# Batch 0's prologue: the second weight-block sum ahead of two token statistics, x's second block ahead of the means' spread

## The chip, the cores and the metric

One Trainium2 chip, one core of it. The metric is the device time of one execution in microseconds (us), the median of several runs. Five engines work side by side, each through its own instruction stream in order: TensorE (PE: matmuls, with PEld for its weight loads), VectorE (DVE), ScalarE (ACT), GpSimd (POOL) and SyncE (SP, which here only issues DMAs). They meet through semaphores: an instruction waits until a semaphore has reached a number, and everything behind it on its engine waits with it.

## What is computed

x has 16 batches of 512 tokens with 512 features. Four normalised or shifted copies of x are scaled, joined to 3072 features per token and put through a two-layer net, whose normalised output is added to x:

```python
h = _ln(x, pw_g[pathway_ids], pw_b[pathway_ids])
h = _ln(h, cp_g[compartment_ids], cp_b[compartment_ids])
t = _ln(x, tm_g[time_steps], tm_b[time_steps])
m = x + _mlp_ln(memory_state, ...)[:, None, :]      # n, r alike, from noise_state, resource_state
s = _ln(x, ms_g[scale_type], ms_b[scale_type])
w = jax.nn.softmax(aw)
cat = jnp.concatenate([w[0]*h, w[1]*t, w[2]*m, w[3]*n, w[4]*r, w[5]*s], axis=-1)
return x + _mlp_ln(cat, int_W1, int_b1, int_W2, int_b2, int_g, int_be)
```

Since m, n and r all hold x itself, the kernel adds up their three blocks of int_W1, weighted with w, into one block that multiplies x.

## The kernel before

Every large matmul is made of float32r operands split in a high and a low part, three matmuls for one product (high by high, high by low, low by high). The features of the joined input come in 16 rows of 128, k = 0 to 15. Rows 0 to 3 are x with the summed weights, the rest are t, s and h. A batch is one turn of `chunk`; batch 0 has a `first_chunk` of its own on each engine, in which the weights are also loaded, summed, scaled and split. The order on each engine is the order in which its code is written out; no scheduler moves anything.

The part that the change touches is the first 30 us of batch 0. What works there on what:

- **The weight sum of block k** (k = 0 to 3, 128 rows each). The three source blocks land in `keep`. ACT's `sum_first(k)` (L691) scales the first of them, DVE's `sum_blocks(k)` (L1149, two instructions) adds the other two, ACT's `sum_high(k)` (L695) rounds the sum to the high part `w1_hi` and DVE's `sum_low(k)` (L1141) takes the rest, `w1_lo`.
- **x turned, in two halves** (two feature rows each). ACT's `x_high(0, i)` (L771) rounds the half i, DVE's `x_low(0, i)` (L936) takes the rest.
- **x's product in block k** on PE: `x_high_part(k)` is four matmuls on x's high part (L1573) and four on its low part (L1576), and waits for `sum_high(k)`; `x_low_part(k)` (L1582, four) waits for `sum_low(k)`.
- **The token statistics of batch 0.** DVE's `x_stats(0, t)` for t = 0 to 3 (L929 and L932) gives mean and variance of the tokens; POOL's `x_rstd(0)` (L520, L522) makes the reciprocal deviations `xrs` once all four are there. ACT puts the means on a diagonal in `mean_diagonal` (L730, four instructions, waits for all four statistics) and the deviations in `dev_diagonal` (L736, waits for `xrs`); DVE's `high_diagonal` (L1124) also waits for `xrs`. PE spreads both over the partitions, `mean_first` (L1557) and `dev_first` (L1562, L1565).
- **What follows from them.** DVE's `scaled_first` (L969) needs `dev_first`; PE's `first_fill(0)` (L1467) needs `scaled_first` and the class table, which ACT rounds and signs (L822, L824) and DVE's `tab_low` (L1136) completes; DVE's `centre_tile(f)` (L960) needs `mean_first`.
- `warm(n)` (L1552) is n matmuls of 128 columns whose result nobody reads, with `WARM = (24, 7)` for the two places where they stand.

Behind `x_low_part(3)` PE goes on with three small nets (`nets_hidden` L1410, `nets_output` L1435), whose weight tiles SP loads through six staging buffers (L428), each released by the matmul that read the tile before it. In the trace the summed weights `w1_raw`, `w1_hi` and `w1_lo` are named w_raw, w_hi and w_lo.

Of the kernel before, what the change touches and what calls it, by code (L numbers as in the profile page):

```python
# [9 lines left out]
TT = TOKENS // P  # L10
# [17 lines left out]

FILLS0, FILLS = 2 * FT + 2, 4

WARM = (24, 7)

# [8 lines left out]
def build(nc, x, xp, xT, ids, pid, small, small_at, tabs, rows, net_vecs, pw, cp, W1s, W2s, int_W1, int_W2, out):  # L43
# [15 lines left out]
    with ExitStack() as ctx:  # L59
# [285 lines left out]
        def by_tiles(cols):  # L345

            return cols.rearrange("q (g t i) -> q t g i", t=TT, i=32)
# [336 lines left out]
        def _(act):  # L684
# [4 lines left out]
            def sum_first(k):  # L689
                act.wait_ge(sum_in[k], 16)  # L690
                act.activation(w1_raw[:, k, :], keep[:, NETS * k, :], ACT.Copy, scale=w_mix[:, 2:3]).then_inc(sum_begun, 1)  # L691
# [34 lines left out]
            def mean_diagonal():  # L726

                act.wait_ge(xaggr, TT)
                for t in range(TT):
                    act.activation(by_tiles(mean_on)[:, t, :, :], ident.rearrange("q (g i) -> q g i", i=32), ACT.Copy,  # L730
                                   scale=xmv[:, t, 0:1]).then_inc(mean_diag, 1)

            def dev_diagonal():
                act.wait_ge(xrs_done, 1)
                for t in range(TT):
                    ins = act.activation(by_tiles(dev_on)[:, t, :, :], ident.rearrange("q (g i) -> q g i", i=32), ACT.Copy,  # L736
                                         scale=xrs[:, t:t + 1])
                ins.then_inc(dev_diag, 1)
# [28 lines left out]
            def x_high(b, i):  # L767
                act.wait_ge(xT_half_in if isinstance(b, int) and b == 0 and i == 0 else xT_in, 16 * (b + 1))

                wait(act, used, 6 * (b - 1) + 5 + i)  # L770
                act.activation(cat_hi[:, slot(i), :, :], xc[:, 2 * i:2 * i + 2, :], ACT.Copy).then_inc(x_hi_done, 1)  # L771
# [42 lines left out]
            sum_high(0)  # L814
            sum_first(1)
            x_high(0, 1)
            mean_diagonal()
            sum_high(1)
            sum_first(2)
            dev_diagonal()  # L820
            act.wait_ge(table_in, 16)
            act.activation(class_tab[:, :], tab_raw, ACT.Copy).then_inc(tab_rounded, 1)  # L822
# [97 lines left out]
        def _(dve):  # L920
# [5 lines left out]
            def x_stats(b, t):  # L926
                if t == 0:
                    dve.wait_ge(x_in, 16 * (b + 1))
                dve.bn_stats(xst[:, t, :], x_sb[:, t, :]).then_inc(xstat, 1)  # L929
                dve.wait_ge(xstat, TT * b + t + 1)  # L930
                dve.nop(nofuse=True)
                dve.bn_aggr(xmv[:, t, :], xst[:, t, :]).then_inc(xaggr, 1)  # L932
# [194 lines left out]
            def high_diagonal():  # L1127

                dve.wait_ge(xrs_done, 1)
                dve.nop(nofuse=True)  # L1130
                diagonal(dev_high, xrs[:, :]).then_inc(high_diag, 1)

            def tab_low():
                dve.wait_ge(tab_hi_done, 1)

                dve.scalar_tensor_tensor(class_tab[:, :], tab_raw, tab_rest, class_tab[:, :].bitcast(f32),  # L1136
                                         ALU.mult, ALU.add).then_inc(tables_ready, 1)
# [6 lines left out]
            def sum_blocks(k):  # L1144
                dve.wait_ge(sum_begun, k + 1)
                if k == 0:
                    dve.wait_ge(sum_more_in[k], 16)
                for j in (1, 2):
                    dve.scalar_tensor_tensor(w1_raw[:, k, :], keep[:, NETS * k + j, :], w_mix[:, 2 + j:3 + j], w1_raw[:, k, :],  # L1149
                                             ALU.mult, ALU.add).then_inc(sum_done, 1)  # L1150
                    dve.wait_ge(sum_done, 2 * k + j)
# [66 lines left out]
            def first_chunk():  # L1218
                class_columns()
                sum_blocks(0)  # L1220
                x_low(0, 0)
                sum_low(0)
                for t in range(TT):
                    x_stats(0, t)
                sum_blocks(1)
                x_low(0, 1)
                high_diagonal()
                sum_low(1)
                sum_blocks(2)
                tab_low()  # L1230
                sum_low(2)
                scaled_first()
                centre_tile(0)
                sum_blocks(3)
                ts_mult(0, 0)
                sum_low(3)
                w_low(4)
                w_low(5)
                ts_low(0, 0)
                centre_tile(1)  # L1240
                ts_mult(0, 1)
                w_low(6)
                w_low(7)
                centre_tile(2)
                ts_low(0, 1)
                onehot_first()
                centre_tile(3)
                w_low(8)
                w_low(9)

                dve.wait_ge(tables_ready, 1)
                y_mul(0, 0)
                y_mul(0, 1)
                ts_mult(0, 2)
                y_mul(0, 2)
                y_mul(0, 3)
                ts_low(0, 2)
                w_low(10)
                w_low(11)
                y_add(0, 0)  # L1260
                ts_mult(0, 3)
                y_add(0, 1)
                ts_low(0, 3)
                y_add(0, 2)
                y_add(0, 3)
                w_low(12)
                for t in range(TT):
                    y_norm(0, t)
                for t in range(TT):
                    x_stats(1, t)  # L1270
                w_low(13)
                h_low(0, 0)
                nets_stats()
                w_low(14)
                w_low(15)
                turn_stats(1)
                h_low(0, 1)
                class_rows()
                nets_norm()
                x_low(1, 0)  # L1280
                x_low(1, 1)
                for t in range(TT):
                    y_mul(1, t)
                onehot_next(1)
                centre(1)
                scaled_next(1)
                y_add(1, 0)
                y_add(1, 1)
# [115 lines left out]
        def _(pe):  # L1404
# [149 lines left out]
            def mean_first():  # L1554

                pe.wait_ge(mean_diag, TT)
                pe.matmul(mean_ps, sel_all, mean_on, start=True, stop=True).then_inc(mean_spread, 1)  # L1557

            def dev_first():

                pe.wait_ge(dev_diag, 1)
                pe.matmul(dev_ps, sel_all, dev_on, start=True, stop=False)  # L1562
                pe.wait_ge(sel_ready, 3)
                pe.wait_ge(high_diag, 1)
                pe.matmul(dev_ps, sel_less, dev_high, start=False, stop=True).then_inc(dev_spread, 1)  # L1565
# [12 lines left out]
            def x_low_part(k):  # L1578
                hi = cat_hi[:, slot(k // 2), k % 2, :]
                pe.wait_ge(sum_lo_done, k + 1)  # L1580
                for h in range(FT):
                    ins = pe.matmul(hid_ps[:, h, :], w1_lo[:, k, h * P:(h + 1) * P], hi, start=False, stop=False)  # L1582
                if k % 2:
                    ins.then_inc(used, 1)
# [49 lines left out]
            def first_chunk():  # L1634
                pe.wait_ge(sel_ready, 1)
                warm(WARM[0])
                x_high_part(0)
                x_low_part(0)
                warm(WARM[1])
                mean_first()  # L1640
                x_high_part(1)
                x_low_part(1)
                dev_first()
                x_high_part(2)
                first_fill(0)
                x_low_part(2)
                x_high_part(3)
                x_low_part(3)
                nets_hidden()
                first_fill(1)  # L1650
                pair(0, 2)
                nets_hidden_turn()
                first_fill(2)
                pair(0, 3)
                first_fill(3)
                for i in range(6):
                    nets_output(i)
                pair(0, 4)
                pair(0, 5)
                for i in range(6, NETS * FT):  # L1660
                    nets_output(i)
                fill_h(0, 0)
                for i in range(6):
                    class_sum(i)
                fill_h(0, 1)
                for i in range(6, MODS):
                    class_sum(i)
                last_pairs(0, 0)
                nets_turn()
                last_pairs(0, 1)  # L1670
                for i in range(NETS * FT):
                    batch_sum(i)
                last_pairs(0, 2)
                batch_turn()
                last_pairs(0, 3)
# [120 lines left out]
```

## Time and profile before

| what | value |
|---|---|
| median of 3 runs | 944.74 us (943.46 to 945.62) |
| the profiled execution's own time | 943.69 us |
| its span, first to last instruction | 942.0 us |
| mean granted TensorE clock | 0.998 of full speed |
| PE busy | 930.0 us, 99% |
| DVE busy | 803.6 us, 85% |
| ACT, POOL busy | 276.4 us, 437.8 us |

The span is counted from the first instruction to the last; 1.7 us of the execution's own time lie around it. Busy time of PE counts matmuls back to back, with modelled ends. The clock column of the profile gives the TensorE clock that was granted, as a share of full speed. Times in the trace are microseconds from the start of the span.

### The profile page before, as it was taken

The numbers are of one execution on the slowest core, as the hardware profiler recorded it, in microseconds if no ns is written. First come the engines' busy times: TensorE is split into PE (matmuls) and PEld (weight loads), VectorE is DVE, ScalarE is ACT, GpSimd is POOL, SyncE is SP. The second block draws the span as 40 slices with busy tenths as digits, with TensorE's granted clock in tenths as the row PEclk, the third lists the DMA queues.
The fourth block names the chain that finished last, engine by engine and source line by source line (L and its number), as shares of the span: only waits on it lengthen the run. The fifth ranks groups of instructions, "written<-read, shape, count | busy, mean of one in ns | idle before, by whom it ended". The sixth has DMA issues, their size and how long they took to land.

```text
span 942.0 us, 13618 instructions
## 1 busy us (share of the span) xinstructions
PE 930.0 (99%) x4219; PEld 747.7 (79%) x4219; DVE 803.6 (85%) x1171; ACT 276.4 (29%) x353; POOL 437.8 (46%) x620
## 2 busy tenths in 40 slices
PE   8999999999999999999999999999999999999996
PEld 7677887878888787887878888787888878788785
DVE  7989998888888888888988889888888888888665
ACT  5635133241321313231241412323132231323211
POOL 3355463554445364454545346355444536445022
PEclk9999999999999999999999999999999999999999
DMA  9974677657475674856667475664847567475331
GB/s 324 368 266 148 204 178 233 180 148 232 132 231 138 235 178 118 246 149 212 155 184 218 115 243 140 228 179 139 233 141 228 139 224 185 119 239 150 87 84 64
DMA packets 98994, 174.56 MB, mean 185 GB/s; under 512 B 11552, under 2 KB 50464, under 8 KB 95008
## 3 DMA queue, kind: packets, MB, share of 16 engines
q0 software_dynamic: 22976, 66.07, 28.6%
q1 hardware_dynamic: 44032, 91.87, 28.1%
q10 hardware_dynamic: 31968, 16.39, 6.0%
q8 instruction: 9, 0.15, 0.1%
q14 instruction: 9, 0.07, 0.0%
HBM read 141.54 MB, written 32.75 MB: 185 GB/s over the span
## 4 chain that ended last, share of the span: by engine, by line
PE 94%; DVE 2%; DMA 2%; SPq 0%; issue 0%; ACT 0%; POOL 0%; DVEq 0%; POOLq 0%
PE hid_ps L1515 25%; PE hid_ps L1516 24%; PE hid_ps L1517 24%; PE o_ps L1616 3%; PE o_ps L1614 3%; PE made_ps L1616 3%; PE made_ps L1614 3%; PE made_ps L1615 3%; PE o_ps L1615 3%; PE made_ps L1467 1%; DMA stage_more<-res_W 1%; DMA keep<-int_W 1%; DVE w_raw L1149 1%; PE hid_ps L1522 0%; SPq L428 0%; PE o_ps L1435 0%
## 5 line engine op out<-in xcount | busy, mean ns | idle before, releaser
L1515 PE MATMUL hid_ps<-cat_hi,w_hi 128*128 128x512 f32 x1008 | 396.6, 393 | 0.0
L1516 PE MATMUL hid_ps<-cat_lo,w_hi 128*128 128x512 f32 x1008 | 392.7, 390 | 0.0
L1517 PE MATMUL hid_ps<-cat_hi,w_lo 128*128 128x512 f32 x1008 | 392.4, 389 | 0.0
L1515 PEld LDWEIGHTS hid_ps<-cat_hi,w_hi 128*128 128x128 f32 x1008 | 189.1, 188 | 49.8 <-issue 11.1
L1517 PEld LDWEIGHTS hid_ps<-cat_hi,w_lo 128*128 128x128 f32 x1008 | 189.2, 188 | 40.2
L1516 PEld LDWEIGHTS hid_ps<-cat_lo,w_hi 128*128 128x128 f32 x1008 | 189.3, 188 | 38.2
L567 POOL DMA_INDIRECT pw_rows<-pw,path_now x64 | 89.9, 1405 | 117.9 <-DVE y_sb L1055 101.8
L775 ACT ACTIVATE cat_hi<-v_ring 128x1024 fp32r<-128x1024 f32 x64 | 66.7, 1059 | 132.7 <-issue 77.9
L588 POOL DMA_DIRECT2D r_sb<-x x60 | 56.7, 946 | 101.4 <-DVE r_sb L1118 92.9
L574 POOL DMA_INDIRECT pw_rows<-cp,class_now x64 | 79.3, 1239 | 35.8 <-DVE y_sb L1030 18.7
L801 ACT ACTIVATE z_sb<-hid_ps,batch_bias 128x512 f32<-128x512 f32 x64 | 43.9, 692 | 168.3 <-PE hid_ps L1517 168.3
L1014 DVE TENSOR_TENSOR cat_lo<-v_ring,cat_hi 128x1024 fp32r<-128x1024 f32 x64 | 76.7, 1200 | 8.0 <-ACT cat_hi L775 8.0
L783 ACT ACTIVATE cat_hi<-v_ring 128x1024 fp32r<-128x1024 f32 x30 | 31.9, 1062 | 170.2 <-DMA v_ring<-h_turned 170.2
L520 POOL TENSOR_TENSOR fve<-fmv,eps_col 128x1 f32<-128x1 f32 x64 | 23.7, 370 | 108.7 <-DVE fmv L1074 96.2
L771 ACT ACTIVATE cat_hi<-xc 128x1024 fp32r<-128x1024 f32 x32 | 33.9, 1061 | 136.8 <-PE hid_ps L1517 136.3
L1118 DVE SCALAR_TENSOR_TENSOR r_sb<-o_sb,frs,rows_bc 128x512 f32<-128x512 f32 x60 | 45.7, 762 | 24.1 <-issue 13.4
L1009 DVE TENSOR_TENSOR v_ring<-made_ps,xc 128x1024 f32<-128x1024 f32 x34 | 41.5, 1221 | 28.3 <-PE made_ps L1467 28.2
L522 POOL TENSOR_TENSOR frs<-fve,minus_half 128x1 f32<-128x1 f32 x64 | 53.3, 833 | 5.0
L1036 DVE SCALAR_TENSOR_TENSOR y_sb<-y_sb,xrs,pw_rows 128x512 f32<-128x512 f32 x64 | 47.6, 743 | 4.5 <-issue 4.5
L520 POOL TENSOR_TENSOR xve<-xmv,eps_col 128x4 f32<-128x4 f32 x16 | 4.7, 293 | 98.4 <-DVE xmv L932 98.4
L1076 DVE SCALAR_TENSOR_TENSOR o_sb<-o_sb,fmv,rows_bc 128x512 f32<-128x512 f32 x60 | 45.6, 759 | 2.1
L1614 PE MATMUL made_ps<-w_hi,hid_hi 128*128 128x512 f32 x120 | 46.7, 389 | 0.0
(177 smaller groups left out, 1368.0 us busy)
## 6 DMA issues: line engine op xcount, KB each, us to landing
x_sb<-xp SPq DMA_DIRECT2D x16, 1024.0 KB, 5.2
out<-r_sb SPq DMA_DIRECT2D x63, 256.0 KB, 2.1
xc<-xT SPq DMA_DIRECT2D x15, 1024.0 KB, 8.3
h_turned<-y_sb ACTq DMA_DIRECT2D x60, 256.0 KB, 6.7
r_sb<-x POOLq DMA_DIRECT2D x60, 256.0 KB, 4.1
v_ring<-h_turned SPq DMA_DIRECT2D x60, 256.0 KB, 3.3
stats_bc<-token_stats SPq DMA_DIRECT2D x120, 64.0 KB
ids_sb<-ids SPq DMA_DIRECT2D x16, 256.0 KB, 5.2
```

The lines of the kernel that those rows point to most:

```text
L522: pool.tensor_tensor(rs[:, cols], ve[:, cols], minus_half[:, cols], ALU.pow).then_inc(rs_sem, 1)
L567: pool.indirect_dma_start(pw_rows[:, t, :], None, pw[:, :], bass.IndirectOffsetOnAxis(ap=path_now[:, t:t + 1], axis=0)).then_inc(rows_in[t ...
L574: pool.indirect_dma_start(pw_rows[:, t, 0:D], None, cp[:, :], bass.IndirectOffsetOnAxis(ap=class_now[:, t:t + 1], axis=0)).then_inc(class_ ...
L588: pool.dma_start(r_sb[:, t, :], x_out_v[b][:, t, :], accum_op=ALU.add).then_inc(added[t], 16)
L775: act.activation(cat_hi[:, slot(TS0 + j), :, :], v_ring[:, slot(TS0 + j), :, :], ACT.Copy).then_inc(ts_hi_done, 1)
L1014: dve.tensor_tensor(cat_lo[:, slot(TS0 + j), :, :], v_ring[:, slot(TS0 + j), :, :], cat_hi[:, slot(TS0 + j), :, :].bitcast(f32), ALU.subtr ...
L1515: pe.matmul(acc, w1_hi[:, k, cols], hi, start=start, stop=False)
L1516: pe.matmul(acc, w1_hi[:, k, cols], lo, start=False, stop=False)
L1517: return pe.matmul(acc, w1_lo[:, k, cols], hi, start=False, stop=stop)
L1614: pe.matmul(acc, hid_hi[:, k, cols], w2_hi[:, k, :], start=(k == 0), stop=False)
L1615: pe.matmul(acc, hid_lo[:, k, cols], w2_hi[:, k, :], start=False, stop=False)
L1616: ins = pe.matmul(acc, hid_hi[:, k, cols], w2_lo[:, k, :], start=False, stop=(k == FT - 1))
```

## The change

Three engines get their batch 0 in another order, and the second warm row is five matmuls for seven. POOL's and SP's streams stay as they are.

```diff
-WARM = (24, 7)
+WARM = (24, 5)
...
             sum_high(0)
             sum_first(1)
             x_high(0, 1)
-            mean_diagonal()
             sum_high(1)
             sum_first(2)
+            mean_diagonal()
             dev_diagonal()
...
                 sum_low(0)
-                for t in range(TT):
-                    x_stats(0, t)
+                x_stats(0, 0)
+                x_stats(0, 1)
                 sum_blocks(1)
                 x_low(0, 1)
-                high_diagonal()
+                x_stats(0, 2)
+                x_stats(0, 3)
                 sum_low(1)
                 sum_blocks(2)
+                high_diagonal()
                 tab_low()
...
                 warm(WARM[1])
-                mean_first()
                 x_high_part(1)
                 x_low_part(1)
+                mean_first()
+                x_high_part(2)
                 dev_first()
-                x_high_part(2)
                 first_fill(0)
```

DVE, from the second weight sum on; the two statistics that leave the place ahead of it are the rows L929 and L932 that come in behind `x_low(0, 1)` (L936).

```order
 L1149 SCALAR_TENSOR_TENSOR w_raw<-keep,small_sb,w_raw 128x512 x2
 L936 TENSOR_TENSOR cat_lo<-xc,cat_hi 128x1024
-L1124 TENSOR_TENSOR cat_lo<-small_sb,xrs 128x4x4x32
+L929 BN_STATS xst<-x_sb 128x6
+L932 BN_AGGR xmv<-xst 128x2
+L929 BN_STATS xst<-x_sb 128x6
+L932 BN_AGGR xmv<-xst 128x2
 L1141 TENSOR_TENSOR w_lo<-w_raw,w_hi 128x512
 L1149 SCALAR_TENSOR_TENSOR w_raw<-keep,small_sb,w_raw 128x512 x2
+L1124 TENSOR_TENSOR cat_lo<-small_sb,xrs 128x4x4x32
 L1136 SCALAR_TENSOR_TENSOR class_tab<-y_sb,small_sb,class_tab 128x512
```

The last two statistics now stand behind the second weight sum and the second x half, and `high_diagonal` behind the third weight sum.

ACT of the changed kernel, from the second half of x to the third weight block's high part.

```order
L771 ACTIVATE cat_hi<-xc 128x1024 [waits xT_in]
L695 ACTIVATE w_hi<-w_raw 128x512 [waits sum_done]
L691 ACTIVATE w_raw<-keep,small_sb 128x512 [waits sum_in2]
L730 ACTIVATE v_ring<-small_sb,xmv 128x4x32 [waits xaggr]
L730 ACTIVATE v_ring<-small_sb,xmv 128x4x32 x3
L736 ACTIVATE v_ring<-small_sb,xrs 128x4x32 [waits xrs_done]
L736 ACTIVATE v_ring<-small_sb,xrs 128x4x32 x3
L822 ACTIVATE class_tab<-y_sb 128x512 [waits table_in]
L824 ACTIVATE class_tab<-class_tab,small_sb 128x512 [waits tab_rounded]
L695 ACTIVATE w_hi<-w_raw 128x512 [waits sum_done]
```

Only the L730 rows moved: before, they stood between L771 and the first L695. In both kernels the last row, `sum_high(2)`, stands behind the two diagonals and the table.

PE of the changed kernel, from the second warm row on; line numbers here are two higher than before (L1575 is L1573 of before, L1578 is L1576, L1584 is L1582, L1559 is L1557, L1564 and L1567 are L1562 and L1565).

```order
L1554 MATMUL o_ps<-v_ring 128x128 x5
L1575 MATMUL hid_ps<-cat_hi,w_hi 128x512 x4
L1578 MATMUL hid_ps<-cat_lo,w_hi 128x512 x4
L1584 MATMUL hid_ps<-cat_hi,w_lo 128x512 x4
L1559 MATMUL o_ps<-v_ring 128x512
L1575 MATMUL hid_ps<-cat_hi,w_hi 128x512 x4
L1578 MATMUL hid_ps<-cat_lo,w_hi 128x512 x4
L1564 MATMUL o_ps<-v_ring 128x512
L1567 MATMUL o_ps<-cat_lo 128x512
L1469 MATMUL made_ps<-scaled,class_tab 128x512 x2
L1584 MATMUL hid_ps<-cat_hi,w_lo 128x512 x4
L1575 MATMUL hid_ps<-cat_hi,w_hi 128x512 x4
```

Before, `mean_first` (now L1559) stood straight behind the warm row, and `dev_first` (L1564, L1567) ahead of the third block's L1575 and L1578.

## Rows read from the trace of the kernel before

**Rows 1.** The page: span, and busy time of PE with share and instructions.
```profile
span 942.0 us, 13618 instructions
PE 930.0 (99%) x4219; PEld 747.7 (79%) x4219; DVE 803.6 (85%) x1171; ACT 276.4 (29%) x353; POOL 437.8 (46%) x620
```

**Rows 2.** Waits of PE from 62 us to the end: total, times, longest.
```profile
PE o_ps L1441 <- DVE net_h L1205: 0.5, 1, 0.5
```

**Rows 3.** Timeline of PE: start, duration, line, operands, count, [idle before <- releaser].
```profile
13.21 1.72 PE L1552 MATMUL o_ps<-v_ring 128*128 128x128 f32 x14
16.34 1.12 PE L1557 MATMUL o_ps<-v_ring 128*128 128x512 f32 x2 [1.41 <-ACT v_ring L730]
...
20.06 1.02 PE L1562 MATMUL o_ps<-v_ring 128*128 128x512 f32 x2
20.52 0.80 PE L1565 MATMUL o_ps<-cat_lo 128*128 128x512 f32 x1
21.15 1.09 PE L1573 MATMUL hid_ps<-cat_hi,w_hi 128*128 128x512 f32 x4
22.08 1.08 PE L1576 MATMUL hid_ps<-cat_lo,w_hi 128*128 128x512 f32 x4
23.09 0.50 PE L1467 MATMUL made_ps<-scaled,class_tab 32*128 32x512 f32 x2
...
25.13 1.20 PE L1573 MATMUL hid_ps<-cat_hi,w_hi 128*128 128x512 f32 x4 [0.42 <-ACT w_hi L695]
```

**Rows 4.** Timeline of DVE, same columns.
```profile
8.10 1.54 DVE L1149 SCALAR_TENSOR_TENSOR w_raw<-keep,small_sb,w_raw 128x512 f32<-128x512 f32 x2 [0.34 <-DMA keep<-int_W]
...
14.03 0.66 DVE L929 BATCH_NORM_STATS2 xst<-x_sb 128x6 f32<-128x512 f32 x1
14.80 0.18 DVE L932 BATCH_NORM_AGGREGATE xmv<-xst 128x2 f32<-128x6 f32 x1
14.90 1.50 DVE L1149 SCALAR_TENSOR_TENSOR w_raw<-keep,small_sb,w_raw 128x512 f32<-128x512 f32 x2
16.44 1.22 DVE L936 TENSOR_TENSOR cat_lo<-xc,cat_hi 128x1024 fp32r<-128x1024 f32 x1
17.58 0.68 DVE L1124 TENSOR_TENSOR cat_lo<-small_sb,xrs 128x512 fp32r<-128x512 f32 x1
...
21.62 0.74 DVE L969 SCALAR_TENSOR_TENSOR scaled<-ids_sb,small_sb,o_ps 128x512 fp32r<-128x512 int32 x1
```

**Rows 5.** Timeline of ACT, same columns.
```profile
12.55 0.72 ACT L691 ACTIVATE w_raw<-keep,small_sb 128x512 f32<-128x512 f32 x1 [2.25 <-DMA keep<-int_W]
13.84 1.06 ACT L771 ACTIVATE cat_hi<-xc 128x1024 fp32r<-128x1024 f32 x1 [0.56 <-DMA xc<-xT]
...
17.59 1.27 ACT L736 ACTIVATE v_ring<-small_sb,xrs 128x128 f32<-128x128 f32 x4
18.76 0.61 ACT L822 ACTIVATE class_tab<-y_sb 128x512 fp32r<-128x512 f32 x1
19.41 0.73 ACT L824 ACTIVATE class_tab<-class_tab,small_sb 128x512 fp32r<-128x512 f32 x1
...
24.45 0.63 ACT L695 ACTIVATE w_hi<-w_raw 128x512 fp32r<-128x512 f32 x1 [2.15 <-DVE w_raw L1149]
```

**Rows 6.** Timeline of POOL, same columns.
```profile
15.15 0.52 POOL L520 TENSOR_TENSOR xve<-xmv,eps_col 128x4 f32<-128x4 f32 x1 [10.83 <-DVE xmv L932]
15.75 1.53 POOL L522 TENSOR_TENSOR xrs<-xve,minus_half 128x4 f32<-128x4 f32 x1
```

**Rows 7.** All instructions of line 522: shortest/median/longest in ns, first and last start.
```profile
L522 POOL TENSOR_TENSOR xrs<-xve,minus_half x16: 1049/1050/1528, 15.8 to 834.1; 128x4 f32<-128x4 f32 x16
```

**Rows 8.** Timeline of PE at the small nets, same columns as rows 3.
```profile
45.18 1.04 PE L1435 MATMUL o_ps<-stage_more,net_hidT 128*32 128x512 f32 x2 [0.67 <-DMA stage_more<-res_W]
```

**Rows 9.** The chain that ended last: start, duration, what; the load behind that wait.
```profile
32.69 12.45 DMA stage_more<-res_W
```

**Rows 10.** One-microsecond stretches at the span's end: PE busy (instructions), granted clock, DMA.
```profile
934.00:935.00 1.00, 0.93 (x5) 1.00 0.00 0
...
938.00:939.00 1.00, 0.00 (x0) 0.99 0.59 198
```

## The prediction, made blind

> **What bounds the kernel now.** I read the page first: PE is busy for 930.0 us of a span of 942.0 [rows 1]. Then the waits of PE: from 62 us to the end only one of 0.5 us is left [rows 2], so batches 1 to 15 run at the speed of the matmuls, and whatever PE loses or wins before that is lost or won at the end, one for one. All that a new order in batch 0 can touch is PE's idle time in the first 46 us. The timeline of PE shows it: 1.41 us ahead of the means' spread at 16.34, 0.42 ahead of x's fourth block at 25.13 [rows 3], and 0.67 at 45.18, where a tile of the small nets has not landed [rows 8].
>
> The timeline of DVE then says what that 25.13 hangs on. From 8.10, where it waited for the first blocks, to the fourth weight sum, DVE has no row with idle time ahead of it [rows 4]: it is full. `x_high_part(3)` waits for `sum_high(3)`, that for `sum_blocks(3)`, and between `scaled_first` at 21.62 and PE's start at 25.13 lie 3.51 us of just this chain (scaled_first, centre_tile(0), the two additions, ACT's rounding) [rows 3, 4]. The change takes no work from DVE ahead of `sum_blocks(3)`; it puts the same instructions in another order. So 25.13 can't come earlier. It can only stay, or come later if DVE is made to wait.
>
> **The change, step by step.**
>
> *What it wins.* ACT's scaling of the second block is done at 12.55 + 0.72 = 13.27, and DVE, with two statistics instead of four ahead, has just arrived. The sum takes 1.54, to 14.87 [rows 4, 5]. x's second half is rounded at 13.84 + 1.06 = 14.90, `sum_high(1)` follows in 0.63, and PE starts 0.05 later: 14.93 + 0.68 = 15.61, where today it stands idle until 16.34 [rows 3, 5]. The fewer warm matmuls (4 of 14 records of 1.72 us, about 0.5 us) only widen a gap, and cost nothing.
>
> *What it puts off.* On DVE `x_low(0, 1)` starts at 14.93 and holds it for 17.58 - 16.44 = 1.14, to 16.07. Then the two late statistics, 14.90 - 14.03 = 0.87 each: the last one starts at 16.94. Today the last one starts at 14.03 and POOL answers 1.12 later, at 15.15, and has `xrs` at 15.75 + 1.53 = 17.28, which is 2.13 after its start [rows 4, 6]. In the changed kernel: 16.94 + 1.12 + 2.13 = 20.19. It comes 2.9 us later than now.
>
> *Who stands behind it.* ACT is in order, and `dev_diagonal` waits for `xrs` with the class table and `sum_high(2)` queued behind. Now it starts at 17.59, straight behind other work. Then: 20.22, plus 1.17 for the diagonal (18.76 - 17.59), 0.65 for the first table copy (19.41 - 18.76), 0.65 for the second by the same spacing: `sum_high(2)` starts at 22.69 and PE can have it 0.68 later, 23.37 [rows 5]. PE has finished `x_low_part(1)` and `mean_first` at about 20.0 (`sum_low(1)` is behind the statistics too, at 17.8 to 18.5) and stands idle for 3.4 us ahead of `x_high_part(2)`, which now began at 21.15.
>
> *What is late next.* PE no longer has `dev_first` behind it: it comes after the eight matmuls of `x_high_part(2)`, 2 x 0.93 = 1.86 (22.08 - 21.15), so at 25.23, and gives the spread after 0.46 + 0.80 = 1.26, at 26.49 [rows 3]. DVE's `scaled_first` starts at 26.53, against 21.62. All the rest of DVE's queue stands behind it, `sum_blocks(3)` in it. The 3.51 us from there to PE's fourth block are unchanged: 26.53 + 3.51 = 30.04, against 25.13. **That is 4.91 us later**. DVE is the proof from the other side: it now waits some 2 us for the table (tab_low, which needs ACT at 22.8) and some 2.3 for the spread, and had waited for nothing.
>
> *What gives some back.* PE comes to the small nets 4.9 us later too, at some 49.4, and the tile that made it wait has landed at 45.18. Its load is issued when a matmul of `nets_hidden` has released a buffer, so SP's issue moves from 32.69 to 37.6; but it took 12.45 us because others were ahead of it, and these drain meanwhile, so it lands at or soon after 45.2 [rows 8, 9]. I take the whole 0.67 off. Bound: nothing of it, if it lands 12.45 after its issue, at 50.0. The later waits of DVE and ACT hang on PE and move with it.
>
> The sum: 4.91 - 0.67 = 4.24. The profiled execution took 943.69, so 947.9. It lies 1.05 below the median of 944.74; by that the sum is 949.0. The profile can't say whether the slower runs lost their time in that DMA wait (then 947.9 holds for all) or elsewhere (then 949.0). I take the middle, 948.4.
>
> *The term that is least sure* is POOL's 2.13. The median of the sixteen roots is 1.05, this one took 1.53 [rows 7], beside DVE additions whose inputs both lie in SBUF [rows 4, 6]. In the changed kernel it runs beside `sum_low(1)` and `sum_blocks(2)`, of the same kind, so I keep 1.53. Bounds: 1.05, 0.5 us less at the end; or the root held until `sum_blocks(2)` has ended (18.44 + 1.53 = 19.97) and 1.05 from there, 21.02, 0.8 us more. The Trainium skill, SBUF — State Buffer, "SBUF: two separate sides", gives a rule for this: VectorE's instructions with two SBUF inputs and GpSimd's share a port pair under an exclusive lock, and the loser "fully blocks". By that rule the sum would be the upper bound, 5.1 for 4.24; by the row, where the root ended although DVE ran such instructions without a break, it stays 4.24.
>
> **The rivals.**
>
> *The clock falls.* A gap of 3.4 us, with gaps of 1.0 to 1.2 before it and 0.9 and 1.2 behind, is new. Nothing in the present prologue comes near: 1.41 us, in a span whose mean granted clock is 0.998. At the end of the span the last matmul ends at 934.93 and the granted clock leaves 2.4 GHz at about 939, after some 4 us [rows 3, 10]. If it falls ahead of `x_high_part(2)`, this part and `dev_first` run at the 1.2 GHz level and take twice 1.86 + 1.26, 3.1 us more on the chain: 951.5. The Trainium skill, TensorE: Matmul & The Clock Gate, "What's actually happening", says of it: "the default state is throttled, and activity releases the throttle". By this rule the long gap is the place where that would happen; the end of this trace agrees, the gap of 1.41 us shows no fall. I give it 13 in 100.
>
> *The DMA is the real bound, and nothing is lost (the other side).* If the nets' tile landed at 49.4 or later in either kernel, PE would resume at one time in both, and the result would be 943.7 to 944.7. The DMA engines' backlog speaks for it: 12.45 us for 256 KB [rows 9]. It decides at 2.4 us: landing that much later than 45.18 it would swallow half of the loss and bring the time within 0.2%. Against it, PE waited 0.67, no more [rows 8]. 6 in 100.
>
> *It does what it is meant to, and the time falls.* PE's second block comes earlier and the gap of 1.41 closes; this helps only if the fourth block comes earlier too, and with DVE full from 8.10 on [rows 4] the best is today's 25.13. Beyond that 0.67 at the nets could go, which makes 943.0 at the very best, within what can be told apart. 2 in 100, above all for what I have not seen.
>
> **How the numbers follow.** The chain above has 79 in 100. Its own range: from 943.69 + 4.24 - 0.5 - some 0.3 of rounding in the spacings = 947.1, with 0.6 less for the scatter of runs, 946.5; up to 944.74 + 4.91 + 0.8 = 950.5. The range that holds 8 in 10 has to reach towards the clock's case: 946.4 to 951.0. What is left out is most of the clock's case, the DMA's and the last. A measurement of this kernel can tell about 0.2% (1.9 us) from no change: slower by more than that has the chain and the clock, 0.79 + 0.13, less 0.01 for losses shrunk to less; within it 0.07; faster 0.02.
>
> **What the changed profile would show.** On ACT, L736 with a wait of about 1 us on POOL's `xrs`, starting near 20.2, and L695 of the third block at 22.7. On DVE, idle time ahead of L1136 (about 2 us, on ACT) and of L969 (about 2.3 us, on PE). On PE, the second block at 15.6, a gap of over 3 us that ends at 23.4, and the fourth block at 30.0. At the nets no wait on `stage_more`. Batches 1 to 15 unchanged. I am wrong if `xrs` is ready before 18 us, if ACT doesn't hold `sum_high(2)`, or if PE waits at the nets for 2 us and more.

## The result, and the profile after

The changed kernel takes **948.33 us** (median of 7 runs, 946.66 to 949.82), the kernel before 944.14 us in the same session (7 runs, 943.18 to 945.62): a ratio of 1.0039, 95% interval 1.003 to 1.0048. It is slower by 4.2 us, 0.4%; forecast were 948.4 us, from 946.4 to 951.0.

The profiled execution of the changed kernel took 946.66 us, the least of its seven runs, with a span of 944.9 us. So it shows 3.0 us of the loss, not 4.2. The page's head, then the waits of PE over the whole span (total, times, longest):

```profile
span 944.9 us, 13609 instructions
PE 927.9 (98%) x4215; PEld 745.7 (79%) x4215; DVE 804.5 (85%) x1171; ACT 276.4 (29%) x353; POOL 459.2 (49%) x620
```

```profile
PE hid_ps L1575 <- ACT w_hi L695: 6.5, 4, 2.6
PE o_ps L1554 <- POOL v_ring L596: 1.1, 1, 1.1
PE hid_ps L1584 <- DVE w_lo L1141: 0.9, 1, 0.9
PE made_ps L1469 <- DVE scaled L969: 0.9, 1, 0.9
PE o_ps L1443 <- DVE net_h L1205: 0.5, 1, 0.5
```

The wait on the nets' load is gone, four waits on ACT's rounding of the weight blocks make 6.5 us, and two new ones hang on DVE. The timeline of PE, to be held against [rows 3]:

```profile
10.09 1.20 PE L1575 MATMUL hid_ps<-cat_hi,w_hi 128*128 128x512 f32 x4 [1.76 <-ACT w_hi L695]
...
15.28 1.19 PE L1575 MATMUL hid_ps<-cat_hi,w_hi 128*128 128x512 f32 x4 [1.05 <-ACT w_hi L695]
...
18.32 1.20 PE L1584 MATMUL hid_ps<-cat_hi,w_lo 128*128 128x512 f32 x4 [0.93 <-DVE w_lo L1141]
19.35 1.02 PE L1559 MATMUL o_ps<-v_ring 128*128 128x512 f32 x2
22.96 1.19 PE L1575 MATMUL hid_ps<-cat_hi,w_hi 128*128 128x512 f32 x4 [2.59 <-ACT w_hi L695]
...
24.91 1.02 PE L1564 MATMUL o_ps<-v_ring 128*128 128x512 f32 x2
25.37 0.79 PE L1567 MATMUL o_ps<-cat_lo 128*128 128x512 f32 x1
27.07 0.50 PE L1469 MATMUL made_ps<-scaled,class_tab 32*128 32x512 f32 x2 [0.91 <-DVE scaled L969]
...
29.78 1.19 PE L1575 MATMUL hid_ps<-cat_hi,w_hi 128*128 128x512 f32 x4 [1.07 <-ACT w_hi L695]
```

Executions start up to 0.3 us apart (the first small load lands at another moment), so I compare distances: from the start of PE's first x block to that of the fourth. It is 29.78 - 10.09 = **19.69 us**. In the kernel before, the timeline of PE has the first block here:

```profile
10.36 1.20 PE L1573 MATMUL hid_ps<-cat_hi,w_hi 128*128 128x512 f32 x4 [0.75 <-ACT w_hi L695]
```

There the distance is 25.13 - 10.36 = **14.77**. The loss on the chain is 4.92 us. Its links, in the timelines of POOL, of ACT and of DVE:

```profile
18.39 1.41 POOL L522 TENSOR_TENSOR xrs<-xve,minus_half 128x4 f32<-128x4 f32 x1
```

```profile
19.84 1.28 ACT L736 ACTIVATE v_ring<-small_sb,xrs 128x128 f32<-128x128 f32 x4 [0.84 <-POOL xrs L522]
21.02 0.61 ACT L822 ACTIVATE class_tab<-y_sb 128x512 fp32r<-128x512 f32 x1
21.67 0.72 ACT L824 ACTIVATE class_tab<-class_tab,small_sb 128x512 fp32r<-128x512 f32 x1
22.29 0.61 ACT L695 ACTIVATE w_hi<-w_raw 128x512 fp32r<-128x512 f32 x1
```

```profile
22.42 0.75 DVE L1136 SCALAR_TENSOR_TENSOR class_tab<-y_sb,small_sb,class_tab 128x512 fp32r<-128x512 f32 x1 [1.84 <-ACT class_tab L824]
...
26.27 0.75 DVE L969 SCALAR_TENSOR_TENSOR scaled<-ids_sb,small_sb,o_ps 128x512 fp32r<-128x512 int32 x1 [2.49 <-PE o_ps L1567]
```

The root is ready at 19.80 instead of 17.28, the third block's high part starts at 22.29 behind it, and DVE, which had no wait here, has waits of 1.84 and 2.49.

At the nets the changed kernel gives back more than was thought. Its `nets_output` group, to be held against [rows 8]:

```profile
46.80 0.50 PE L1469 MATMUL made_ps<-scaled,class_tab 32*128 32x512 f32 x2
47.23 1.48 PE L1437 MATMUL o_ps<-r_sb,net_hidT 128*32 128x512 f32 x7
48.12 0.60 PE L1437 MATMUL o_ps<-stage_more,net_hidT 128*32 128x512 f32 x2
48.55 0.59 PE L1437 MATMUL o_ps<-r_sb,net_hidT 128*32 128x512 f32 x1
48.55 0.60 PE L1437 MATMUL o_ps<-stage_more,net_hidT 128*32 128x512 f32 x2
...
60.23 1.48 PE L1437 MATMUL o_ps<-r_sb,net_hidT 128*32 128x512 f32 x7
```

The two groups of the trace of before, from its timeline of PE:

```profile
42.60 1.47 PE L1435 MATMUL o_ps<-r_sb,net_hidT 128*32 128x512 f32 x7
...
57.27 1.48 PE L1435 MATMUL o_ps<-r_sb,net_hidT 128*32 128x512 f32 x7
```

From the first group's start to the second's it takes 60.23 - 47.23 = 13.00 us now, and took 57.27 - 42.60 = 14.67. That is **1.67 us** back, where the wait row said 0.67. The matmuls of three nets run beside each other: each leaves two records, and three records, one of each net, take a step of 0.43 us. The tile that came late in the kernel before had its two records alone (0.98 us, from 45.18 to the next matmul at 46.16), so it cost that time as well as the wait. So 4.92 - 1.67 = 3.25, less 0.27 of the start, is the 3.0 of the two profiled executions.

### The profile page after: what moved, and what is told of

Same layout as the page of the kernel before. It is cut to its first block, busy times and chain, and to the rows that moved or that the text cites. A ratio compares the mean times of both kernels' runs of the same rounds, so it can differ in the third digit from the quotient of the medians.

```text
span 944.9 us, 13609 instructions
## 1 busy us (share of the span) xinstructions
PE 927.9 (98%) x4215; PEld 745.7 (79%) x4215; DVE 804.5 (85%) x1171; ACT 276.4 (29%) x353; POOL 459.2 (49%) x620
## 4 chain that ended last, share of the span: by engine, by line
PE 96%; DVE 1%; DMA 1%; ACT 1%; POOL 0%; SPq 0%; issue 0%; POOLq 0%; DVEq 0%
PE hid_ps L1517 25%; PE hid_ps L1518 24%; PE hid_ps L1519 24%; PE o_ps L1618 3%; PE o_ps L1616 3%; PE made_ps L1616 3%; PE made_ps L1618 3%; PE made_ps L1617 3%; PE o_ps L1617 3%; PE made_ps L1469 1%; DMA xc<-xT 1%; PE o_ps L1437 0%; PE hid_ps L1524 0%; PE o_ps L1426 0%; PE o_ps L1425 0%; PE o_ps L1453 0%
## 5 line engine op out<-in xcount | busy, mean ns | idle before, releaser
L574 POOL DMA_INDIRECT pw_rows<-cp,class_now x64 | 88.1, 1377 | 40.2 <-DVE y_sb L1030 22.9
L771 ACT ACTIVATE cat_hi<-xc 128x1024 fp32r<-128x1024 f32 x32 | 33.8, 1060 | 133.1 <-PE hid_ps L1519 132.6
L522 POOL TENSOR_TENSOR frs<-fve,minus_half 128x1 f32<-128x1 f32 x64 | 66.6, 1041 | 5.0
L1617 PE MATMUL made_ps<-w_hi,hid_lo 128*128 128x512 f32 x120 | 46.7, 389 | 0.0
```

The lines of the kernel that those rows point to most:

```text
L522: pool.tensor_tensor(rs[:, cols], ve[:, cols], minus_half[:, cols], ALU.pow).then_inc(rs_sem, 1)
L574: pool.indirect_dma_start(pw_rows[:, t, 0:D], None, cp[:, :], bass.IndirectOffsetOnAxis(ap=class_now[:, t:t + 1], axis=0)).then_inc(class_ ...
L1617: pe.matmul(acc, hid_lo[:, k, cols], w2_hi[:, k, :], start=False, stop=False)
```

## The experiments

The theory was that of the prediction: the late root and ACT's queue hold the third block, `dev_first` behind it holds DVE, and the nets' wait gives some back. The rivals: that the late statistics alone are the cause; and, for the 1.2 us by which the loss of the medians (4.2) exceeds that of the profiles (3.0), that the clock falls in some executions.

**e1: the largest gap filled.**

```diff
                 mean_first()
+                warm_gap(9)      # nine matmuls of 128 columns into dev_ps
                 x_high_part(2)
```

> The changed kernel with nine more matmuls of 128 columns, read by nobody, between mean_first and x_high_part(2), about 2.2 us of work in a gap that measured 2.59 us. Theory 'late chain': PE only waits there, so x's fourth block starts as in the changed kernel, 19.7 us after the first (14.8 in the kernel before), and the profile and the median stay at about 948.3, clock or no clock. Rival 'the clock falls in some executions': the seven runs of the changed kernel show mean granted clocks of 0.999 (946.66 us) down to 0.995 (949.82 us); if the gap makes the clock fall in these, filling it keeps the clock at 0.997 to 0.999 in all runs and the median comes down to about 946.7.

Median 946.83 us (6 runs: four from 946.64 to 946.87, two at 948.39 and 948.42); distance 19.69 us. The chain is as long as in the changed kernel, so PE's idle time there costs nothing as such. The runs hint at the clock, but don't settle it: the mean granted clock was 0.997 in all six. It also counts the fall behind the last matmul, and so tells little of the prologue.

**e2: ACT's sum_high(2) ahead of dev_diagonal.**

```diff
             mean_diagonal()
+            sum_high(2)
             dev_diagonal()
...
-            sum_high(2)
             nets_join()
```

> The changed kernel with ACT's sum_high(2) taken from behind the class table to ahead of dev_diagonal. Theory 'late chain': sum_high(2) then waits only for sum_blocks(2), about 19.7 us on this trace's scale, the third block on PE starts near 20.4 instead of 22.96 and dev_first near 22.3; scaled_first is then held by the table (tab_low near 22.9) and starts near 24.2 instead of 26.27. The fourth block starts about 2.1 us earlier than in the changed kernel, 17.6 us after the first, and the median is about 2 us below that of the changed kernel (about 946.3). Rival 'the two late statistics are the whole of it': no gain, because xrs is as late as before, 19.7 us between the first and the fourth block.

Median 944.84 us (11 runs, 944.59 to 947.35); distance 27.80 - 10.24 = 17.56 us, 2.13 less, as expected. The median is 1.5 us below the 946.3 expected, which was counted from the changed kernel's 948.3; counted from its fastest runs (946.7, see e8) 2.13 less is 944.6. The root is as late as in the change, so the late statistics alone are not the cause: it is what stands behind them on ACT. In the execution that was profiled (947.32 us, one of the slowest) the fourth block ran at 1.2 GHz, its first four matmuls in 1.87 us instead of the 1.02 of the first trace (29.78 to 30.80), as its timeline of PE shows:

```profile
27.80 2.07 PE L1575 MATMUL hid_ps<-cat_hi,w_hi 128*128 128x512 f32 x4 [1.10 <-ACT w_hi L695]
29.67 1.91 PE L1578 MATMUL hid_ps<-cat_lo,w_hi 128*128 128x512 f32 x4
```

**e3: DVE's order put back.**

```diff
-                x_stats(0, 0)
-                x_stats(0, 1)
+                for t in range(TT):
+                    x_stats(0, t)
                 sum_blocks(1)
                 x_low(0, 1)
-                x_stats(0, 2)
-                x_stats(0, 3)
+                high_diagonal()
                 sum_low(1)
                 sum_blocks(2)
-                high_diagonal()
```

> The changed kernel with DVE's order put back to that of the kernel before (all four statistics and high_diagonal in their old places), ACT and PE as changed. Theory 'late chain', with its second half, that dev_first now stands behind x_high_part(2) and ACT's table behind mean_diagonal: sum_high(2) at about 21.3, the third block at 22.0, dev_first at 23.9, scaled_first at 25.2, the fourth block 18.3 us after the first, that is 1.4 us less than in the changed kernel and 3.5 more than before; median about 947. Rival 'the two late statistics are the whole of it': the loss vanishes, 14.8 us between the blocks, median 944.

Median 946.01 us (11 runs, 945.42 to 947.16), where 947 was expected; distance 28.88 - 10.06 = 18.82 us, where 18.3 was expected. With the statistics as early as before, 4.05 of the 4.92 us on the chain stay (some 0.5 of them, an estimate from the starts of its rows, from blocks that ran at 1.2 GHz in this execution): ACT's and PE's new order is bad without DVE's too. The rival that the statistics are the whole of it is refuted from both sides.

**e4: DVE's new order alone, in the kernel before.**

> The kernel before with DVE's new order alone (two statistics behind x_low(0,1), high_diagonal behind sum_blocks(2)); ACT, PE and the warm row as before. Theory 'late chain': ACT's mean_diagonal, which stands ahead of sum_high(1), now waits for the late statistics to about 17.9, sum_high(1) to 19.1, DVE's third weight sum starts at 20.4, dev_first on PE at 22.6, scaled_first at 24.2, the fourth block 17.3 us after the first, 2.6 more than before; after what the small nets give back, 1 to 2 us slower than before. Rival 'the late statistics are the whole of it': the full loss, 19.7 us between the blocks.

Median 946.30 us against 944.76 (11 runs, 944.66 to 947.30). Distance 29.38 - 10.17 = 19.21 us, 1.9 more than expected. The timeline of PE and a stretch of the windows view (stretch, length, PE busy, granted clock, DMA share, GB/s) say why:

```profile
19.15 1.86 PE L1559 MATMUL o_ps<-v_ring 128*128 128x512 f32 x2 [4.38 <-ACT v_ring L730]
20.02 2.70 PE L1575 MATMUL hid_ps<-cat_hi,w_hi 128*128 128x512 f32 x4
22.51 1.24 PE L1578 MATMUL hid_ps<-cat_lo,w_hi 128*128 128x512 f32 x4
```

```profile
20.00:22.00 2.00, 2.00 (x5) 0.50 1.08 306
```

`mean_first` starts at 19.15, straight behind `mean_diagonal`, which was expected to end at 19.1. Then, behind 4.38 us of idle time, the granted clock is 0.50, and the first four matmuls of the second block take 2.49 us to the next row, where the same row took 1.11 in the trace of before (17.12 to 18.23). From `mean_first` to `dev_first` it takes 24.50 - 19.15 = 5.35 us, and took 20.06 - 16.34 = 3.72. With these 1.63 us taken off, 17.6 are left for the 17.3 expected. The same off the 946.34 us of this execution leaves 944.7, and three of the 11 runs lie at 944.66 to 944.87.

**e5: dev_first back ahead of x_high_part(2), all else as changed.**

```diff
                 mean_first()
-                x_high_part(2)
                 dev_first()
+                x_high_part(2)
                 first_fill(0)
```

> The changed kernel with dev_first back ahead of x_high_part(2) on PE, nothing else. Theory 'late chain': dev_first waits for dev_diagonal only and starts near 21.2 instead of 24.9; scaled_first is then held by the class table and sum_low(2), near 23.8 instead of 26.3; the fourth block starts 17.3 us after the first instead of 19.7, and the median falls by about 2.4 us against the unaltered change. Rival 'dev_first's place is immaterial, the late xrs sets it all': 19.7 us as in the unaltered change.

```profile
10.14 1.19 PE L1575 MATMUL hid_ps<-cat_hi,w_hi 128*128 128x512 f32 x4 [1.26 <-ACT w_hi L695]
...
27.24 1.19 PE L1575 MATMUL hid_ps<-cat_hi,w_hi 128*128 128x512 f32 x4 [0.58 <-issue]
```

Median **944.25 us** (11 runs, 944.09 to 944.48), ratio to before 0.9997 (0.9988 to 1.0006), no difference. Distance 27.24 - 10.14 = 17.10 us, where 17.3 was expected. This one line is worth 2.59 us of chain and 4.0 us of median (948.28 in e8, of the same session), where 2.4 was expected: e5 has no upper group of runs, and against the lowest group of the changed kernel (946.7) it is 2.5. The 2.33 us of chain that are left are about what the nets give back.

**e8, e10 and e11: the changed kernel again, three more traces.**

> The changed kernel once more, unaltered, on one chip with the other kernels of this call. Theory 'late chain, and a clock that sometimes falls in its gaps': the PE rows stand within 0.3 us of the first profile as long as the clock holds (19.7 us from the first to the fourth block of x); if it falls in this execution, the records show 1.2 GHz somewhere between 20 and 34 us and the time is 1 to 3 us longer. Over all its runs those of the lowest mean clock (0.994 to 0.996) are the slowest. Rival 'the scatter is the nets' loads alone': clock and time have nothing to do with each other.

> The changed kernel unaltered, one look at its trace. Theory: if its own time is near 946.7, no row between 16 and 72 us shows the 1.2 GHz level; if it is near 948.3 or 949.7, such rows stand there, and they account for the 1.6 or 3 us. Rival: a slow execution with all rows at 2.4 GHz and the time lost in a wait.

> The same kernel, a second look, with the same expectations as the first: 1.2 GHz rows between 16 and 72 us where its own time is above 948, none where it is near 946.7.

e8: median 948.28 us (5 runs: 946.67, 946.80, 948.28, 948.29, 949.71). Together with the first seven and the two single executions e10 and e11, six of 14 runs lie at 946.7 to 947.1, five at 948.3 to 948.5, three at 949.5 to 949.8. The three slowest have the lowest mean granted clocks (0.994 and 0.995); the other two groups can't be told apart by it (0.996 to 0.997, and 0.997 to 0.999).

The traces of e8 (946.67) and e11 (946.85) show the distance of the first one (19.68 and 19.81). In e11 the clock holds, as in the first. In e8 it fell, but earlier than was expected, and the time is none the longer. Its timeline of PE and its windows (columns as for e4):

```profile
10.14 1.37 PE L1575 MATMUL hid_ps<-cat_hi,w_hi 128*128 128x512 f32 x4 [1.95 <-ACT w_hi L695]
```

```profile
12.00:14.00 2.00, 2.00 (x6) 0.50 1.01 385
14.00:16.00 2.00, 2.00 (x15) 0.90 1.07 392
```

Most of the first block ran at the 1.2 GHz level, and the second block began at 15.61 instead of 15.28. The third waits for ACT anyway, so nothing of this reached the end. A fall is thus not enough: it counts where it comes.

e10 took **949.49 us**, and the same two views of it show the difference:

```profile
29.84 2.07 PE L1575 MATMUL hid_ps<-cat_hi,w_hi 128*128 128x512 f32 x4 [1.09 <-ACT w_hi L695]
31.71 1.91 PE L1578 MATMUL hid_ps<-cat_lo,w_hi 128*128 128x512 f32 x4
33.42 1.91 PE L1584 MATMUL hid_ps<-cat_hi,w_lo 128*128 128x512 f32 x4
35.26 0.99 PE L1412 MATMUL o_ps<-r_sb,small_sb 128*32 128x512 f32 x2
```

```profile
26.00:28.00 2.00, 1.09 (x5) 1.00 1.06 407
28.00:30.00 2.00, 0.91 (x5) 0.80 1.04 402
30.00:32.00 2.00, 2.00 (x5) 0.50 1.02 394
...
34.00:36.00 2.00, 2.00 (x8) 0.50 1.06 385
```

The fourth block starts where it did (distance 19.69), but the granted clock falls to 0.50 behind the gaps, while PE waits ahead of this block, and stays there for some 6 us: from the fourth block to the nets' first matmul it takes 35.26 - 29.84 = 5.42 us instead of 32.71 - 29.78 = 2.93. That and the little that follows are the 2.8 us above the first profile. No execution of the middle group (948.3 to 948.5) was traced.

**e9: all five gaps filled.**

```diff
-WARM = (24, 5)
+WARM = (24, 9)
...
                 x_high_part(1)
+                warm_gap(3)
                 x_low_part(1)
                 mean_first()
+                warm_gap(10)
                 x_high_part(2)
                 dev_first()
+                warm_gap(3, made_ps[:, 0, 0:P])
                 first_fill(0)
                 x_low_part(2)
+                warm_gap(4)
                 x_high_part(3)
```

> The changed kernel with matmuls of 128 columns, read by nobody, in all five gaps of the prologue: four more in the warm row, three ahead of x_low_part(1), ten ahead of x_high_part(2), three ahead of first_fill(0), four ahead of x_high_part(3). The runs of the changed kernel fall in three heaps, 946.7, 948.3 and 949.7 us. Theory 'the upper heaps are executions in which the clock fell in the prologue': with the gaps filled all runs lie at 946.7 within 0.4 us, and the chain is as long as before, 19.7 us from the first to the fourth block. Rival 'the heaps have another cause': they stay, with a median near 948.3.

Median **946.86 us**, all eight runs from 946.68 to 946.97; distance 29.86 - 10.13 = 19.73. The five gaps are those behind the first block. The one ahead of it stayed, 1.78 us here, and in the trace the clock fell behind it, as in e8, and cost as little:

```profile
12.00:14.00 2.00, 2.00 (x6) 0.50 1.03 390
14.00:16.00 2.00, 2.00 (x15) 0.82 1.05 386
...
28.00:30.00 2.00, 1.80 (x13) 1.00 1.05 409
```

The upper groups are gone while the chain is unchanged. With the trace of e10 this shows that they are the doing of the clock, where it falls late in the prologue: 1.5 us of the changed kernel's median. For the middle group it rests on e9 alone. The Trainium skill, TensorE: Matmul & The Clock Gate, "What's actually happening", has it that idleness brings back the throttled state. These traces agree in so far as every fall seen stands behind idle time: 0.50 granted behind the later gaps in e10, and in e9 only behind the one gap that was left open.

**e6 and e7: three of the nets' first six matmuls some 3 us later**, in the kernel before and in the changed one.

```diff
-                for i in range(6):
+                for i in range(3):
                     nets_output(i)
-                pair(0, 4)
+                pair(0, 4, between=nets_between)   # nets_output(3..5) after its first half
                 pair(0, 5)
-                for i in range(6, NETS * FT):
-                    nets_output(i)
                 fill_h(0, 0)
-                for i in range(6):
+                for i in range(3):
                     class_sum(i)
+                for i in range(6, NETS * FT):
+                    nets_output(i)
+                for i in range(3, 6):
+                    class_sum(i)
```

> The kernel before with three of the first six matmuls of nets_output (the tiles that landed last) put behind the first half of pair(0,4), and the second six behind fill_h(0,0) and the first three class sums. The profile of before showed 0.67 us of wait at this place, but from the third fill (42.17) to pair(0,4) (46.16) it took 1.67 us more than in the changed kernel. Theory 'the wait cost 1.67, since the late tile's matmul also ran alone instead of beside the others': the kernel comes out 1.0 to 1.6 us faster than the kernel before, and its runs scatter less than 942.9 to 945.7. Rival 'it cost what the wait row says': 0.3 to 0.7 us, no less scatter.

> The changed kernel with the same move of the nets' matmuls. Theory: it had no wait at the nets, so its profile and median stay as in the unaltered change of this call, within 0.5 us, and the difference between the two kernels with this move is the whole 4.9 us of the chain: about 4.9 us between them, against 3.0 to 4.2 without it. Rival 'the changed kernel waits at the nets in its slower runs too': its median falls as much as that of the kernel before does.

e6: **942.72 us**, ratio 0.9984 (0.9975 to 0.9993); ten of 11 runs within 942.57 to 942.92, where the kernel before scatters from 942.94 to 945.88. Its distance is unchanged, 24.95 - 10.18 = 14.77. So the scatter of the kernel before comes from that wait, and it costs more in the median than in the one execution profiled; no slower execution of the kernel before was traced. The gain of 1.9 us is above the 1.0 to 1.6 expected, and it is net of what the move costs. From the fourth block's start to `nets_turn` (L1441, which ends the first chain of the nets) it takes 45.11 us in the trace of before, 44.32 in that of e6 and 43.43 in that of the changed kernel, which waits for no load: 0.9 us are lost by the move, 0.3 of them in a new wait of `fill_h(0, 0)` on ACT, from the list of PE's waits:

```profile
PE made_ps L1508 <- ACT y_sb L796: 0.3, 1, 0.3
```

e7: 949.18 us (5 runs, 947.81 to 950.53), 0.9 above e8 of the same session: outside the 0.5 us expected, but by just what the move costs (44.28 from the fourth block to `nets_turn`), with no wait to lose in exchange. Between the medians of e7 and e6 lie 6.5 us, not the 4.9 expected: four of e7's five runs lie 1.1 to 2.7 us above the lowest, as those of the changed kernel's upper groups do. Its lowest run, which was the one traced, less the median of e6 is 5.1 us, and the change without late clock falls (e9) less e6 without its cost is 946.86 - 942.72 + 0.9 = 5.0: the whole 4.9 of the chain comes out when nothing gives back.

**e12: the group kept together, behind the first half of pair(0,4)**, with one class sum ahead of `fill_h(0, 0)`.

> The kernel before with the first six nets_output matmuls kept together and put behind the first half of pair(0,4), and the second six behind fill_h(0,0) and three class sums, one of them ahead of fill_h(0,0). The kernel with the split move lost 0.43 us by running its two halves apart and 0.28 us by a wait of fill_h(0,0) on ACT. Theory 'the nets' wait is the only scatter of the kernel before': this one runs 0.7 us faster than the split move, at about 942.0, with a scatter of 0.4 us or less. Rival: the loads, released later, land too late for the second six, a new wait appears there and the time is 943 or more.

Median **942.33 us**, ratio 0.9981 (0.9972 to 0.9990), 11 runs from 942.22 to 942.55, where 942.0 was expected: faster than both kernels by 2 us and more, and than e6 by 0.4 rather than 0.7. (Its own way from the fourth block to `nets_turn` is 43.90 us, 0.4 less than e6's.) PE has neither a wait for a load nor one on y_sb:

```profile
PE hid_ps L1575 <- ACT w_hi L695: 2.2, 2, 1.8
PE o_ps L1559 <- ACT v_ring L730: 1.4, 1, 1.4
PE o_ps L1554 <- POOL v_ring L596: 1.1, 1, 1.1
PE o_ps L1441 <- DVE net_h L1205: 0.5, 1, 0.5
```

## Why the prediction was right, and where only its total was

*What it wins.* As worked out: PE's second block starts 5.19 us behind the first (15.28 - 10.09); the sum had 15.61 - 10.36 = 5.25.

*What it puts off, who stands behind, what is late next.* Right link by link. With 0.27 added for the earlier start, the root is ready at 20.07 (20.19 was forecast), `sum_high(2)` starts at 22.56 (22.69), the third block at 23.23 (23.37), `scaled_first` at 26.54 (26.53), the fourth block at 30.05 (30.04). The loss was forecast as 4.91 and measured as 4.92, and from `nets_turn` to the end of the span the two kernels take 871.8 and 871.7 us, so batches 1 to 15 are unchanged as forecast. One sign was missed without harm: the gap ahead of `x_high_part(2)` is 2.59 us, where 3.4 and "over 3" were forecast, since PE was through with `mean_first` at 20.6, not 20.0 (`x_low_part(1)` had itself waited 0.93 us for `sum_low(1)`).

The root took 1.41, between the bounds and near the 1.53 that was kept; DVE's additions with two SBUF inputs ran without a break from 18.18 to 19.71 beside it. In e4, where DVE stood idle beside it, it took 1.01. Held until both additions were over it would have ended at 20.8; it ended at 19.80, so the upper bound was not reached. But that bound asked too much of the rule it was taken from. The Trainium skill, SBUF — State Buffer, "SBUF: two separate sides", gives the port pair to whoever starts first "for the whole instruction", and `sum_blocks(2)` is two instructions. Held until the first had ended (18.18 + 0.75 = 18.93), with 1.05 from there, the root would end at 19.98, an estimate: 0.2 from the measured end, so this trace doesn't speak against the rule.

e5 and e2 bear out both halves: take away `dev_first`'s new place or ACT's queue, and 2.6 or 2.1 us of chain are gone. That the fewer warm matmuls cost nothing was not tested by itself; the gap they widen is one of the five that e9 filled.

*What gives some back* is the term that was mis-sized: 0.67 in the sum, 1.67 in the two profiled executions. A wait row gives the idle time of the engine, not what the late tile cost. And it was not a fixed sum: by e6 it cost the kernel before 2.8 us in the median (944.6 - 942.7, and the 0.9 of the move), by e12 2.5 (944.37 - 942.33, and the 0.5 of its move), and 1.7 in the execution that was profiled.

*The clock's fall*, put at 13 in 100, lengthened, by e9 and e10, eight of 14 executions and adds 1.5 us to the median (948.33 for the 946.86 of e9). Two errors thus cancelled. With both terms as measured it is 4.9 - 2.8 + 1.5 = 3.6 (3.9 with the 2.5 of e12), and the medians of the e8 session differ by 3.6 (948.28 - 944.64); the first one had 4.2. The sum had 4.24 with 0.67 and nothing. That 948.4 came within 0.1 us of the median is therefore luck; the 4.9 of the chain is not. The prediction looked for the fall ahead of `x_high_part(2)`, behind the longest gap; in e10 it came later, at the fourth block, behind a row of gaps of 0.9 to 2.6 us, and cost 2.8 us where the rival had 3.1. Where it falls differs from one execution to the next (in e8, e9 and e7 at the first block, where it cost nothing), and the traces don't show what decides it.

*The DMA as the real bound* was the right thing to be wary of: it stood behind the scatter of the kernel before, but held the changed one in none of its four traces.

## What to carry to other kernels

Before an instruction is moved back, look at everything that stands behind its consumers on their engines: here two statistics were put off by 2.9 us, and a weight block that has nothing to do with them came late, since ACT had it in the queue behind the deviations. The costliest line was on PE (2.6 us of chain): eight matmuls that DVE did not need yet were put ahead of `dev_first`, whose result DVE, a full engine, waits for. And where the runs of a kernel scatter, look for a wait on a load near its start: moving its consumer by 3 us was worth 0.2% here (2.0 us in e12), more than the 1.7 that the prediction gave the reordering at its very best.

## What the runs showed of the hardware

- Gaps of 0.9 to 2.6 us in a row were followed by the 1.2 GHz level in e10, 0.50 granted for some 6 us, and gaps of 0.9 to 1.3 us in e2; by the groups of run times it was so in eight of 14 executions of the changed kernel. A gap of 4.4 us was followed by it in e4's trace, one of 2.6 us in e3's, and the one ahead of the first block in e7's, e8's and e9's (1.77, 1.95 and 1.78 us).
- The same gap ahead of the first block was not followed by it in the first trace and in e11 (1.76 and 1.67 us), nor was the one of 1.41 us in the kernel before, nor those of 0.4 to 1.3 us in e5 (11 runs within 0.4 us). The length of a gap alone doesn't tell.
- A fall cost nothing where the next work waited for another engine anyway (e8, 946.67 us), and 2.8 us where PE's work was what the rest waited for (e10, 949.49 us).
- Matmuls of 128 columns that nobody reads, in the five gaps behind the first block, kept all eight executions of e9 within 0.3 us and delayed nothing.
- Three nets' matmuls of 32 rows out run beside each other, a step of 0.43 us for three records; the late tile's two records, alone, took 0.98 us to the next row. A late tile cost its wait and this.
- POOL's root of 128x4 took 1.41 us beside DVE additions with two SBUF inputs, and 1.01 in e4, where DVE was idle.
